# A scan whose drive is written over B's row in PSUM, with C's rows by transfer and the low half on GpSimd

## The reference

```
# layer 0, mixer: a selective scan, N = 16 states per channel
B, C  = xn @ W_bc  (16 columns each)
delta = softplus(xn @ W_dt @ W_dtproj + b)
h_n[t] = exp(delta[t] * A_n) * h_n[t-1] + delta[t] * xn[t] * B_n[t]     # along 256 tokens
y[t]   = sum_n C_n[t] * h_n[t] + D * xn[t]
# layer 1, mixer: per token, 16 heads of 8: softmax(Q) @ (softmax(K^T) @ V)
# both layers, experts: 8 experts 128 -> 512 -> 128, exact gelu, the best 2 per token
# by a softmax gate, their weights renormalised; layer 1 has biases and gamma/beta in front
```

## Time and profile before

| | |
|---|---|
| median of 3 runs | 1031.66 us |
| profiled execution | 1025.65 us, its span 1023.9 us |
| VectorE busy | 849.8 us, 83% |
| TensorE busy | 690.9 us, 67% |
| ScalarE busy | 531.4 us, 52% |
| GpSimd busy | 464.7 us, 45% |
| first instructions to the scan | 0 to 121 us |
| scan of layer 0 with 72 blocks | 121 to 545 us |
| results in, lead-in to layer 1 | 545 to 690 us |
| heads of layer 1 with 72 blocks | 690 to 1000 us |
| last results in, output | 1000 to 1024 us |

### The profile page before, as it was taken

The page is one execution under the profiler, slowest core; times in us unless marked ns, Lnnn a source line. Parts: engine busy times, 40 slices in busy tenths (PEclk is TensorE's granted clock), DMA queues, the critical chain, the costliest instruction groups (busy, mean ns, idle before and its releaser), DMA issues. The chain is left out here.

```text
span 1023.9 us, 17950 instructions
## 1 busy us (share of the span) xinstructions
PE 690.9 (67%) x4708; PEld 438.0 (43%) x4708; DVE 849.8 (83%) x1900; ACT 531.4 (52%) x1221; POOL 464.7 (45%) x451
## 2 busy tenths in 40 slices
PE   1975176787888988888882046247697697697670
PEld 0432022355354535454541036135576476475550
DVE  4899999997999999999894866846967967966967
ACT  2568422277757575858531272026755755755720
POOL 1566375544252525354421046344565465564530
PEclk9955578798999999999997555559897897897875
DMA  8241000011010101010104102000111111010108
GB/s 251 83 134 31 0 1 1 19 29 30 20 32 21 35 17 35 22 34 24 30 20 129 50 1 82 1 19 27 30 33 32 28 33 32 29 34 29 33 10 246
DMA packets 49889, 44.68 MB, mean 44 GB/s; under 512 B 8098, under 2 KB 41320, under 8 KB 49796
## 3 DMA queue, kind: packets, MB, share of 16 engines
q1 hardware_dynamic: 36356, 23.58, 7.8%
q0 software_dynamic: 9216, 17.85, 6.4%
q10 hardware_dynamic: 4224, 2.10, 0.7%
HBM read 28.82 MB, written 15.73 MB: 44 GB/s over the span
## 5 line engine op out<-in xcount | busy, mean ns | idle before, releaser
L421 POOL DMA_INDIRECT results<-res,pair_of x144 | 155.6, 1081 | 311.5 <-DVE res L1081 257.4
L415 POOL DMA_INDIRECT xrow<-rows,row_of x144 | 170.3, 1182 | 65.0 <-issue 50.7
L527 ACT ACTIVATE arena<-ph,b 128x128 f32<-128x128 f32 x432 | 123.7, 369 | 90.4 <-PE ph L723 43.7
L1120 DVE TENSOR_TENSOR_SCAN work<-decay,work 128x256 f32<-128x256 f32 x256 | 163.0, 679 | 1.1
L698 PE MATMUL py<-work,idf 128*128 128x512 f32 x256 | 140.9, 639 | 2.8 <-DVE work L1129 2.8
L519 ACT COPY xrT<-px 128x256 f16<-128x256 f16 x144 | 53.4, 371 | 169.5 <-PE px L707 131.8
L1096 DVE TENSOR_TENSOR arena<-arena 128x512 f16<-128x512 f32 x144 | 98.7, 685 | 39.5 <-ACT arena L533 37.2
L739 PE MATMUL po<-w,arena 128*128 x576 | 123.0, 293 | 0.0
L679 PE MATMUL pb<-parts,pick 96*128 96x512 bf16 x256 | 84.4, 412 | 51.5 <-DVE work L1129 39.4
L738 PE MATMUL po<-w,arena 128*128 x576 | 114.3, 233 | 0.0
L515 ACT ACTIVATE decay<-big,avec 128x512 f32<-128x512 f32 x128 | 81.7, 712 | 44.3 <-DVE work L1120 44.1
(11 more groups left out here) (196 smaller groups left out, 1545.6 us busy)
## 6 DMA issues: line engine op xcount, KB each, us to landing
decay<-in_w SPq DMA_DIRECT2D x32, 256.0 KB, 3.5
rows<-rows SPq DMA_DIRECT2D x16, 256.0 KB, 2.3
decay<-results SPq DMA_DIRECT2D x16, 256.0 KB, 3.9
big<-results SPq DMA_DIRECT2D x16, 256.0 KB, 5.0
xrow<-rows,row_of POOLq DMA_INDIRECT x144
results<-res,pair_of POOLq DMA_INDIRECT x144
x<-in_x SPq DMA_DIRECT2D x4, 512.0 KB, 6.1
out<-x ACTq DMA_DIRECT2D x8, 256.0 KB, 4.5
```

Of the source, the lines that this page charges most:

```text
L415: e.indirect_dma_start(xrow[:, b % XR, :], None, rows_dram[l], bass.IndirectOffsetOnAxis(row_of[:, b:b + 1], 0)).then_inc(s_row[b % XR], 16)
L421: e.indirect_dma_start(res_dram[l], bass.IndirectOffsetOnAxis(pair_of[:, b:b + 1], 0), res[:, b % RR, :], None, bounds_check=NRES - 1, oob ...
L527: ins = e.activation(hid[:, b % 2, c * P:(c + 1) * P], hidden(l, b)[:, c * P:(c + 1) * P], ACT.Gelu, bias=b1[:, col(en * HC + (l * NE * HC ...
L1120: ins = e.tensor_tensor_scan(work[:, 2 + n % 2, sl], decay[:, n, sl], work[:, n % 2, sl], 0.0, ALU.mult, ALU.add)
```

## The change

- The drive is written back over B's row in PSUM, in three banks `pb[0..2]` in turn, and the scan reads it there. The scan is one instruction of 512 columns. For that, the decay at each sequence's first token is zero: GpSimd sets these once (`starts`), and ScalarE's exponentials leave them out.
- C's rows no longer come by matmul. In the lead-in ScalarE copies C (c_out) to SBUF, SP stores it to DRAM, and in the scan SP loads each row, spread over 128 partitions, into a ring of four (CR), once the product four states earlier is done.
- The low half of the gelu (split) goes from VectorE to GpSimd, between its transfers. The rings grow: 4 high halves, 3 low halves, 2 PSUM banks for the hidden values.
- `block_down` writes all its products into the same 128 columns, so `block_out` is a copy of 128 columns; it takes 14 matmuls in place of 9.
- `block_turn` and `block_in` take two blocks at once.
- Lags are 0, 2, 2, 5, 6, 7 ticks for turn, up, split, down, out, send; fetches are 4 blocks ahead in place of 6; the drain has 7 ticks in place of 5. In the scan ticks are spread over all 16 states of a group, and the numbers per group change. The exponentials come in two pieces of 8 per group.
- `rows` is a ring of two groups in place of all eight: a cast of group g waits for the store of group g-2. SP's order in the lead-in is, for each group, its rows, its C, then the weights of expert 8 + g.

```diff
-TICKS = ((0, 9, 10, 10, 10, 11, 11, 11), (9,) * GROUPS)
+TICKS = ((0, 7, 10, 11, 11, 11, 11, 11), (9,) * GROUPS)
+WINDOW = 8
+CR = 4
-DRAIN = 5
+DRAIN = 7
-HR = 3
+HR = 4
+LR = 3
-AHEAD = 6
+AHEAD = 4
-        rows = sb("rows", [P, TILES, ROWF], F16)
+        c_ring = sb("c_ring", [P, 2, GC])
+        rows = sb("rows", [P, 2, TG, 2 * D], F16)
-        py = ps("py", [P, GC])
-        px = ps("px", [P, 2 * D], F16)
-        ph = ps("ph", [P, HID])
+        ph = ps("ph", [P, 2, HID])
+        px = ps("px", [P, 2 * GC], F16)
+        starts = decay[:, :, :].rearrange("p n (s t) -> p n s t", t=SLEN)[:, :, :, 0:1]
+        py = pb[:, 3, :]
+        def c_row(at):
+            return c_ring[:, at % CR - 2, :] if at % CR >= 2 else work[:, at % CR, :]
+        def tick_at(g, n):
+            first = LATE if g == 1 else 0
+            here = ticks_of(0, g)
+            for i, tick in enumerate(here):
+                if n == first + (2 * i + 1) * (NS - first) // (2 * len(here)):
+                    return tick
+            return None
 ...                                          # SP
+            for i in range(8):
+                experts(i)
             for l in range(2):
                 for g in range(GROUPS):
                     e.wait_ge(s_rlo, l * GROUPS + g + 1)
                     e.dma_start(rows_dram[l][g * GC:(g + 1) * GC, :].rearrange("(t p) c -> p t c", p=P),
-                                rows[:, g * TG:(g + 1) * TG, :]).then_inc(s_rout, 16)
+                                rows[:, g % 2, :, :]).then_inc(s_rout[g % 2], 16)
+                    if l == 0:
+                        e.wait_ge(s_cT, g + 1)
+                        e.dma_start(c_dram[:, group(g)], c_stage[112:128, g % 2, :]).then_inc(s_cst[g % 2], 16)
+                        experts(8 + g)
 ...
+                    e.wait_ge(s_topw, 1)
+                    for g in range(GROUPS):
+                        for n in range(NS):
+                            at = g * NS + n
+                            if at >= CR:
+                                e.wait_ge(s_prod, at - CR + 1)
+                            e.dma_start(c_row(at), c_dram[n:n + 1, group(g)].to_broadcast([P, GC]))\
+                                .then_inc(s_c[at % CR], 16)
 ...                                          # GpSimd
+            e.wait_ge(s_wlo, 2 * NE)
+            e.memset(starts, 0.0).then_inc(s_zero, 1)
+                def split(b):
+                    at = l * BLOCKS + b
+                    e.wait_ge(s_hh, at + 1)
+                    if at >= LR:
+                        e.wait_ge(s_l2, at - LR + 1)
+                    e.tensor_tensor(hid_l[:, b % LR, :], hid[:, b % 2, :], hid_h[:, b % HR, :], ALU.subtract)\
+                        .then_inc(s_hl, 1)
-                for b in range(BLOCKS):
-                    if b + AHEAD < BLOCKS:
-                        fetch(b + AHEAD)
-                    send(b)
+                for tick in range(BLOCKS + DRAIN):
+                    if tick + AHEAD < BLOCKS:
+                        fetch(tick + AHEAD)
+                    if (b := block_at(tick, 7)) is not None:
+                        send(b)
+                    if (b := block_at(tick, 2)) is not None:
+                        split(b)
 ...                                          # ScalarE
+            def rows_high(l, g):
+ ...
+                if g >= 2:
+                    e.wait_ge(s_rout[g % 2], 16 * (g // 2 + l * GROUPS // 2))
+                e.copy(rows[:, g % 2, :, 0:D], (xf if l else xn)[:, g * TG:(g + 1) * TG, :]).then_inc(s_rhi, 1)
             def decay_of(g, n):
                 e.wait_ge(s_scan, g * NS + (n + 1))
-                e.activation(decay[:, n, :], big[:, group(g)], ACT.Exp, scale=avec[:, n:n + 1]).then_inc(s_a, 1)
+                inner = [v.rearrange("p (s t) -> p s t", t=SLEN)[:, :, 1:SLEN] for v in (decay[:, n, :], big[:, group(g)])]
+                e.activation(inner[0], inner[1], ACT.Exp, scale=avec[:, n:n + 1]).then_inc(s_a, 1)
+            def scan_group(g, expert, due):
+                for n in range(NS):
+                    if (tick := tick_at(g, n)) is not None:
+                        blocks_tick(0, tick, expert)
+                    if n % WINDOW == 0 and 0 < g * NS + n <= (GROUPS - 1) * NS:
+                        due.extend(range(g * NS + n - WINDOW, g * NS + n))
+                    if due and (tick is None or tick % 2 == 0):
+                        for at in due:
+                            decay_of(at // NS + 1, at % NS)
+                        due.clear()
+                        if g > 0:
+                            table_for(ACT.Gelu)
 ...                                          # TensorE
+                at = g * NS + n
+                if at >= 3:
+                    e.wait_ge(s_scan, NS + at - 2)
+                spread(g, n, at % 3, s_bb, 0)
 ...                                          # block_down
-                e.matmul(both, ones_h[:, :], b2_parts[:, bass.ds(en * (2 * D), 2 * D)], start=True, stop=False)
+                for k in range(2):
+                    e.matmul(o, ones_h[:, :], b2_parts[:, bass.ds(en * (2 * D) + k * D, D)], start=(k == 0), stop=False)
                 for c in range(HC):
-                    e.matmul(high, hl, w2_all[:, bass.ds(w, D)], start=False, stop=False)
-                    ins = e.matmul(both, hh, w2_all[:, bass.ds(w, 2 * D)], start=False, stop=(c == HC - 1))
+                    e.matmul(o, hl, w2_all[:, bass.ds(w, D)], start=False, stop=False)
+                    e.matmul(o, hh, w2_all[:, bass.ds(w, D)], start=False, stop=False)
+                    ins = e.matmul(o, hh, w2_all[:, bass.ds(w + D, D)], start=False, stop=(c == HC - 1))
 ...                                          # VectorE
-                e.tensor_reduce(res[:, b % RR, :], po[:, 0:2 * D].rearrange("p (k d) -> p d k", k=2), AX_X, ALU.add)\
-                    .then_inc(s_res, 1)
+                e.tensor_copy(res[:, b % RR, :], po[:, 0:D]).then_inc(s_res, 1)
-                e.tensor_tensor(work[:, n % 2, :], dx, pb[:, n % 2, :], ALU.mult).then_inc(s_bx, 1)
+                e.tensor_tensor(pb[:, at % 3, :], dx, pb[:, at % 3, :], ALU.mult).then_inc(s_bx, 1)
-                for h in range(GC // SLEN):
-                    sl = slice(h * SLEN, (h + 1) * SLEN)
-                    ins = e.tensor_tensor_scan(work[:, 2 + n % 2, sl], decay[:, n, sl], work[:, n % 2, sl],
-                                               0.0, ALU.mult, ALU.add)
-                ins.then_inc(s_scan, 1)
+                e.tensor_tensor_scan(work[:, 2 + n % 2, :], decay[:, n, :], pb[:, at % 3, :],
+                                     0.0, ALU.mult, ALU.add).then_inc(s_scan, 1)
-                e.tensor_tensor(work[:, 4 + n % 2, :], work[:, 2 + n % 2, :], pb[:, 2 + n % 2, :],
+                e.tensor_tensor(work[:, 4 + n % 2, :], work[:, 2 + n % 2, :], c_row(at),
                                 ALU.mult).then_inc(s_prod, 1)
```

247 lines of the change are left out of this document (119 added, 128 removed).

## The result

Four runs of the changed kernel gave 1060.55 us in the median (1054.23 to 1060.76). Four runs of the kernel before on the same chip gave 1032.14 (1031.63 to 1038.28). The ratio is 1.0246, its 95% interval 1.0192 to 1.0301. So the change makes the kernel slower by 28 us. The prediction had it faster by 14.5, and the time lies above its range.

The account below looks back on a forecast made before the run. VectorE was taken to bound scan and second layer, with GpSimd slack to spend; afterwards GpSimd would bind the second layer. Terms for scan, lead-ins, second layer and drains summed to -14.5 us on 1031.66, giving 1017, range 978 to 1050.

Parts of the forecast that it names:

- the hold of the weighs: Scan: GpSimd's splits meet VectorE's weighs about half the time, costing 0.6 on average then, 3.3 us a group.
- the allowance of 1.5: Scan: VectorE (45) and GpSimd (44) wait for each other every block, so a group of 11 blocks takes 46.5 us.
- ScalarE's windows: Scan: each window of 8 exponentials with table loads blocks the gelus for 7.7 us, part of the allowance from 45 to 46.5.
- Copy, scan, drive: VectorE in the scan: 0.20 us for a block's copy, 1.13 for a 512-wide scan, 0.60 for a drive.
- PSUM over PSUM: Slower rival, scan: drives reading and writing one PSUM bank take 0.53 us more each, about 1077 us; chance 0.10.
- C's rows late: Slower rival, scan: late loads of C's rows put 2 us on each state, +60 us or more; chance 0.04.
- First lead-in: Before the scan: late expert weights delay ScalarE's queue and VectorE's routing, +2.5 us (bounds 0 to 4).
- Second lead-in: Before the second layer: ScalarE's casts wait for stores of the two-group ring, all on the path, +9 us (+5 to +12).
- Second layer: Its eight groups: GpSimd binds at 4.3 us a block, a group goes from 37.87 to 38.8, +8 us.
- Behind the scan: After the scan's last group: two more ticks in flight, with sends of 1.3 and splits at GpSimd's pace, +3 us.
- GpSimd over its limit: Slower rival, both layers: a split takes 1.9 us with its issue, 4.8 a second-layer block, 1079 us; chance 0.16.
- GpSimd doesn't bind: Faster rival: scan groups take 43 us and second-layer groups 34, about 962, half way 990; chance 0.22.

Follow-up runs that it names:

- second pair of profiles: The changed kernel and the kernel before, both repeated unedited on the chip of the experiments: medians 1050.32 us (ratio 1.038) and 1014.24 us.

## Why the prediction was wrong

**Two terms of a scan group failed: the hold of the weighs, put at 3.3 us a group, and the allowance of 1.5 for "two queues that wait for each other".** The hold measured 6.9 and the waits 5.6. The forecast group was 41.6 + 3.3 + 1.5, rounded to 46.5; the measured one is 41.7 + 6.9 + 5.6 = 54.2. What is left for the plain work is right to 0.1.

- *The hold.* The mechanism was named, with the rows of 13.94 and of 1.50. The size was not. I took a meeting as a random overlap of 1.15 in 2.33 and a loss of 0.6. But the weigh loses from the hand-over of the split, behind 0.5 to 0.7 of descriptors, and starts again from nothing, so that a long meeting costs 1.4 to 1.6, and a quarter of the weighs had one. Without the descriptors in front it measured 2.7, close to my 3.3: 24 of 80 weighs were held, 4.8 a group, by 0.6 in the mean, where I had 5.5 by 0.6. The bound was in the text: the rule at its worst, 12.7. Between 3.3 and 12.7 I chose the end with the row, and the range then held only a few us of it.
- *ScalarE's windows.* I wrote that a window blocks the gelus for 7.7 us, "about the two ticks of slack that they have", and let the allowance pay. It blocks them for 8.5. What I didn't follow is the queue behind the waiting product: `y_sum`, and behind it the weigh. Nor did I count that TensorE goes on at half the granted clock after it has stood still. Here the text should have named who waits. Without the exponentials the scan is 32 shorter (part of it fewer holds); with short windows 10.
- *Copy, scan, drive.* 0.20 from start to start, 1.13 and 0.60 were forecast. 406.42 to 406.62, 410.35 to 411.48 and 409.75 to 410.35 are exactly these. PSUM over PSUM, a rival at 0.10, falls: a drive that is written over B's row lasts 0.68, as it did into SBUF.
- *C's rows late* (0.04) falls: without the transfers nothing changes.
- *First lead-in,* +2.5: measured +3.4 in the first pair of profiles and nothing in the second, so it isn't shown that the wait forecast there was paid.
- *Second lead-in,* +9: measured +10.6, by the steps forecast. ScalarE's cast of group 2 and GpSimd's subtractions:

```profile
646.43 0.62 ACT L545 CAST rows<-big 128x512 f16<-128x512 f32 x1 [13.15 <-DMA rows<-rows]
```

```profile
630.11 15.04 POOL L410 TENSOR_TENSOR rows<-big,rows 128x512 f16<-128x512 f32 x2 [8.43 <-ACT rows L545]
647.12 2.27 POOL L410 TENSOR_TENSOR rows<-big,rows 128x512 f16<-128x512 f32 x2 [1.97 <-ACT rows L545]
651.34 2.28 POOL L410 TENSOR_TENSOR rows<-big,rows 128x512 f16<-128x512 f32 x2 [1.96 <-ACT rows L545]
```

  The starved subtraction, first of the two in its row, ends at 644.0, its store lands 2.3 later, and pairs follow every 4.2 (forecast 4.5). The earlier trace rows had the whole chain. The casts were only in the way: nothing before the route needs them.
- *Second layer,* +8: measured +0.9 (+2.5 in the second pair of profiles). GpSimd was to bind at 4.3 us a block. Its own work and issue gaps are 3.9, since fetch and send were 1.17 and 1.10 and no dearer than before, and it waits for the rest. So the group of 37.8, not 38.8, was nearly hit with a mechanism that the runs don't bear out. Wide and narrow products come to the same there, as the text had it; in the kernel before, the narrow ones cost 9.7, which it did not price.
- *Behind the scan,* +3: measured +8.1. All runs with the changed order show 22 to 25, before 16 to 17, so this is neither hold nor window. It isn't the split on GpSimd either: with the split back on VectorE it is 23.2. The longer drain (seven ticks) is the likely cause; it wasn't tried apart. At the end +5.3 to the first result, forecast +2, is the same.
- *GpSimd over its limit,* the slower rival at 0.16, gave 1079 by a split of 1.9. It measures 1.21. The time lies half way to it by another way, and in the scan GpSimd has slack: it waited 37.8 us of 200 for ScalarE's casts.
- *GpSimd doesn't bind,* a rival at 0.22: its sum has a slip. "2 x 5 + 3.5 x 5" is 27.5; the 17.5 that was used is the second product alone.

In the scan no engine was the bound alone: of 200 us VectorE was busy for 174, counting the holds, TensorE for 171, GpSimd for 136 and ScalarE for 134. Two engines put at 45 a group each and a third that stops for 8.5 came out at 54.

## What to carry over

When an elementwise instruction moves from VectorE to GpSimd, count VectorE's instructions with two SBUF inputs that remain, and look at what stands ahead of the moved one in GpSimd's queue: behind a descriptor-writing transfer it holds VectorE for the rest of that transfer too, and an empty instruction between them gave back 25 us here. When an engine stops for a window, follow the queue of everyone who waits for it down to the first instruction that the bounding engine needs, and look at the granted clock behind TensorE's idle time. The same columns in more matmuls cost 9.7 us in the second layer of the kernel before, and nothing that shows in that of the changed one.

## What the hardware showed that was not expected

- A weigh that started 0.3 to 0.5 us ahead of a GpSimd subtraction still lost to it and lasted 2.04 to 2.28 us in place of 0.67, if a send ran when it started; with GpSimd drained the 14 with leads of 0.24 to 0.67 lasted 0.66 to 0.69, and none at all over 1.67. That the hand-over decides is my reading of these facts; no record shows the moment. By the Trainium skill (SBUF — State Buffer, Who interferes with whom) the first to issue wins; by the recorded starts it was the second that won behind a send, and the first with GpSimd drained.
- A fetch that started while a weigh was under way took 1.24 (409.43 above). One with VectorE idle took 0.97 (378.15 in the same trace). Why isn't shown.
- A wait costs more than its length where queues are ordered: leaving out the exponentials also took 2 us of holds off each group.
- Before each of the three long waits of the scan TensorE was idle for 3.2 to 3.9 us, and in the stretch that followed the granted clock was 0.5.
